# A new table of places, zero products and first-batch order for a two-layer transformer kernel, and GpSimd's clearing ahead of its first statistics

## The reference, cut to what matters

```python
h = _layernorm(x) * (1 + ca) + sa
x = x + ga * _L0_attn_ref(h, ...)      # scores masked to 0 above the diagonal; a score of 0 becomes NEG_FILL
h = _layernorm(x) * (1 + cb) + sb
x = x + gb * _L0_ffn_ref(h, ...)       # softmax gate, argmax, one of 8 experts, relu
h = _layernorm(x) * (1 + ca) + sa
x = x + ga * _L1_attn_ref(h, ...)      # 16 heads of 8: softmax(q k^T) v, then Wout
h = _layernorm(x) * (1 + cb) + sb
x = x + gb * _L1_ffn_ref(h, ...)       # W1, W2, no activation between
```

## Time and profile before

| | us |
|---|---|
| median of 3 runs | 1714.44 (1712.82 to 1715.45) |
| the profiled execution's own time | 1714.09 |
| its span, first to last instruction | 1712.8 |
| first row maximum (h = -32) | 129.74 |
| first exponential (h = 0) | 177.97 |

### The profile page before, as it was taken

The page is one execution under the profiler, slowest core; times in us unless marked ns, Lnnn a source line. Parts: engine busy times, 40 slices in busy tenths (PEclk is TensorE's granted clock), DMA queues, the critical chain, the costliest instruction groups (busy, mean ns, idle before and its releaser), DMA issues.

```text
span 1712.8 us, 56705 instructions
## 1 busy us (share of the span) xinstructions
PE 1621.6 (95%) x24168; PEld 707.5 (41%) x24168; DVE 1482.1 (87%) x2256; ACT 1368.1 (80%) x1934; POOL 667.8 (39%) x1085
## 2 busy tenths in 40 slices
PE   6998999999999999999999999999999999999998
PEld 3754443344434443334434443334434443323335
DVE  5649988999889998899889998899989998989963
ACT  4443778988899878988899878988899887777784
POOL 2321345445444355444554365344554362102010
PEclk9999999999999999999999999999999999999999
DMA  2111211112120311012110311112110221111101
GB/s 74 52 56 36 63 32 55 33 53 65 56 64 19 97 57 55 28 45 76 58 58 19 89 49 55 46 47 77 42 58 23 74 58 42 52 33 46 37 27 32
DMA packets 83288, 87.22 MB, mean 51 GB/s; under 512 B 9452, under 2 KB 67484, under 8 KB 83036
## 3 DMA queue, kind: packets, MB, share of 16 engines
q1 hardware_dynamic: 82492, 83.07, 16.4%
q10 hardware_dynamic: 544, 0.52, 0.1%
HBM read 61.02 MB, written 21.99 MB: 48 GB/s over the span
## 4 chain that ended last, share of the span: by engine, by line
PE 63%; ACT 16%; DVE 14%; issue 4%; POOL 2%; DMA 1%; SPq 0%; ACTq 0%; POOLq 0%; DVEq 0%
PE pv_psum L809 21%; PE side_psum L537 15%; PE buffer L794 11%; ACT p L1040 10%; DVE row_max L1364 8%; PE buffer L784 7%; PE side_psum L627 2%; PE buffer L537 2%; PE side_psum L594 1%; PE pv_psum L819 1%; ACT o_sb L1049 1%; DVE st_f L1103 1%; ACT p0T L967 1%; POOL sm_f L1394 1%; POOL xn_f L1400 1%
## 5 line engine op out<-in xcount | busy, mean ns | idle before, releaser
L1364 DVE TENSOR_REDUCE row_max<-buffer 128x2 f32<-128x1024 f32 x1024 | 1219.6, 1217 | 118.7 <-PE buffer L784 107.0
L1040 ACT ACTIVATE p<-buffer 128x1024 f32<-128x1024 f32 x1024 | 1043.6, 1026 | 184.2 <-PE buffer L794 171.5
L809 PE MATMUL pv_psum<-p,v 128*9 128x256 f32 x8192 | 575.7, 382 | 4.1 <-ACT o_sb L1049 2.2
L784 PE MATMUL buffer<-k_ops,q_ops 24*128 24x512 f16 x2048 | 397.6, 385 | 29.5 <-ACT p L1040 22.0
L794 PE MATMUL buffer<-q_ops,k_ops 26*128 26x512 f16 x2048 | 397.1, 385 | 4.4 <-DVE row_max L1364 3.1
L809 PEld LDWEIGHTS pv_psum<-p,v 128*9 128x9 f32 x8192 | 155.2, 89 | 234.9 <-issue 150.2
L794 PEld LDWEIGHTS buffer<-q_ops,k_ops 26*128 26x128 f16 x2048 | 96.0, 91 | 350.9 <-issue 244.4
L784 PEld LDWEIGHTS buffer<-k_ops,q_ops 24*128 24x128 f16 x2048 | 96.0, 91 | 147.7 <-ACT p L1040 112.3
L1510 POOL TENSOR_SCALAR nm_parts<-nm 128x16 f16<-128x16 f32 x64 | 17.0, 266 | 351.3 <-DVE nm L1287 351.3
L1495 POOL TENSOR_TENSOR hm<-masks,hT_f 128x1024 f32<-128x1024 bf16 x56 | 120.1, 2150 | 64.0 <-PE side_psum L537 50.8
L537 PE MATMUL side_psum<-we,hm 128*32 128x128 f32 x3648 | 121.0, 274 | 0.0
(11 more groups left out here) (310 smaller groups left out, 1674.5 us busy)
## 6 DMA issues: line engine op xcount, KB each, us to landing
masks<-masks_rows SPq DMA_DIRECT2D x16, 1024.0 KB, 5.7
q_ops<-products SPq DMA_DIRECT2D x256, 48.0 KB
k_ops<-products SPq DMA_DIRECT2D x256, 48.0 KB
attention<-o_sb SPq DMA_DIRECT2D x248, 18.0 KB
x<-in_L_attn_inputs SPq DMA_DIRECT2D x8, 512.0 KB, 4.3
products<-q_parts SPq DMA_DIRECT2D x16, 256.0 KB, 2.2
w_sb<-in_L_ffn_W SPq DMA_DIRECT2D x16, 256.0 KB, 3.2
out<-x SPq DMA_DIRECT2D x16, 256.0 KB, 2.8
```

The lines of the kernel that those rows point to most:

```text
L784: m = e.matmul(buffer[:, hh, :], q_ops[rows, slot, of, i * P:(i + 1) * P], k_ops[rows, slot, of, halves(half)[1]], start=True, stop=True)
L809: m = e.matmul(pv_psum[q:q + VW, half * QUARTER:(half + 1) * QUARTER], v1[b % 2][:, kb, 2 * hp + hh, :], p_sb[n % KEPT][:, hh, part * QUAR ...
L1040: e.activation(p_sb[n % KEPT][:, :, :], unit("exp", n)[0][:, :, :], ACT.Exp, scale=over_scale[n // (2 * PERIOD)]).then_inc(S["exp_done"], 1)
L1364: e.tensor_reduce(mx[pair % 2][:, :, i, half], unit("max", n)[0][:, :, :], axis=AX.X, op=ALU.max).then_inc(S["max_done"], 1)
```

## The change

Only tables change, and the place of four memsets. COUNTED has new values throughout (126 entries before, 122 now); of the other tables these lines show the pattern:

```diff
-SWITCH, LIGHT = 1.2, 6.6
+SWITCH, LIGHT = 0.6, 5.4
 PLACES = """
--15 maxima 0, -7 nm_split 0, -10 nm 0, 0 maxima 1, 1 nm_split 1, 4 nm 1, ...
+-14 maxima 0, -15 nm_split 0, -10 nm 0, 2 maxima 1, -3 nm_split 1, 6 nm 1, ...
...
 ALONE = """
-apply 0 0 1, channels 0 0 0, channels 0 0 1, g0 0 0, gates 0, g0 0 1, ...
+apply 0 0 1, channels 0 0 0, stats 0 0 1 0, channels 0 0 1, gates 0, g0 0 0, g0 0 1, ...
...
@@ gpsimd_program @@
+        for v in (be3[:, :], onehotT[:, :], b2_sb[:, :], gate_sb[:, :, :]):
+            e.memset(v, 0.0).then_inc(S["zero_rows"], 1)
+
         def norm_small(mv, sm, half, signal):
...
-        for v in (be3[:, :], onehotT[:, :], b2_sb[:, :], gate_sb[:, :, :]):
-            e.memset(v, 0.0).then_inc(S["zero_rows"], 1)
         pool.wait_ge(S["in_c"], 48)
```

More of the change, by code:

```diff
@@ L110 @@
 PLACES = """
[L111 to L114, removed]
@@ new lines @@
+3, -112 residual 0 0, -100 stats 0 2 0 0, -99 stats 0 2 0 1, -97 apply 0 2 0, -93 channels 0 2 0, -91 qk1 0 0 0, -64 parts 0 0 0, -85 qk1 0 1 0, -86
+parts 0 1 0, -88 v1 0 0, -133 stats 0 1 1 0, -132 stats 0 1 1 1, -132 apply 0 1 1, -127 channels 0 1 1, -126 wg 0 1, -125 top 0 1 0, -123 top 0 1 1,
+-124 index 0 1 0, -119 index 0 1 1, -118 gating 0 1 0, -119 onehot 0 1, -116 gating 0 1 1, -117 onehotT 0 1, -116 over_gating 0 1, -119 masks_out 0 1,
+-117 masks_load 0 1, -105 hm 0 4, -100 hm 0 5, -100 moe_a 0 4, -99 moe 0 4, -98 hm 0 6, -95 moe_a 0 5, -94 moe 0 5, -83 hm 0 7, -82 moe_a 0 6, -81 moe
@@ L177 @@
-1, index 0 0 0, squares 0, apply 1 0 0, index 0 0 1, times_v 0 7, onehot 0 0, up 0 1, stats 0 1 1 0, gating 0 0 1, stats 0 1 1 1, onehotT 0 0,
-channels 0 1 1, channels 1 0 0, apply 0 1 1, wg 0 1, hm 0 0, limits 0, top 0 1 0, apply 1 0 1, channels 1 0 1, moe_a 0 0, g0 1 0, masks_out 0 0,
-gating 0 1 0, inverse 0, g0 1 1, onehotT 0 1, gating 0 1 1, over_gating 0 0, index 0 1 0, moe 0 0, masks_load 0 0, top 0 1 1, hm 0 1, moe_a 0 1, index
-0 1 1, powers 0, later 1, onehot 0 1, moe 0 1, hm 0 2, hm 0 3, residual 0 0, masks_out 0 1, moe_a 0 2, moe 0 2, masks_load 0 1, moe_a 0 3, moe 0 3,
@@ new lines @@
+exp0 0 6, apply 0 1 0, masks_out 0 0, times_v 0 5, softmax 0 7, scores 0 7 1, transpose_p 0 6 0, channels 0 1 0, transpose_p 0 6 1, stats 1 0 0 0, wg
+0 0, top 0 0 0, stats 1 0 0 1, sums0 0 1, exp0 0 7, times_v 0 6, stats 1 0 1 0, transpose_p 0 7 0, top 0 0 1, index 0 0 0, squares 0, transpose_p 0 7
+1, times_v 0 7, gating 0 0 0, index 0 0 1, gating 0 0 1, onehot 0 0, stats 1 0 1 1, up 0 1, onehotT 0 0, apply 1 0 0, limits 0, channels 0 1 1, stats
+0 1 1 0, channels 1 0 0, channels 1 0 1, g0 1 0, stats 0 1 1 1, apply 0 1 1, apply 1 0 1, gating 0 1 0, inverse 0, hm 0 0, powers 0, wg 0 1, g0 1 1,
@@ new lines @@
+top 0 1 0, index 0 1 0, moe_a 0 0, onehotT 0 1, hm 0 1, top 0 1 1, over_gating 0 0, gating 0 1 1, moe 0 0, v0 1, moe_a 0 1, index 0 1 1, onehot 0 1,
+moe 0 1, hm 0 2, hm 0 3, hm 0 4, residual 0 0, later 1, gates 1, scores 1 0 0, moe_a 0 2, moe 0 2, moe_a 0 3, moe 0 3, stats 0 2 0 0, masks_load 0 0,
+stats 0 2 0 1, moe_a 0 4, hm 0 5, hm 0 6, over_gating 0 1, moe 0 4, softmax 1 0, exp0 1 0, moe_a 0 5, moe 0 5, apply 0 2 0, channels 0 2 0, qk1 0 0 0,
+hm 0 7, masks_out 0 1, moe_a 0 6, moe 0 6, scores 1 1 0, qk1 0 1 0, moe_a 0 7, masks_load 0 1, softmax 1 1, parts 0 0 0, parts 0 1 0, moe 0 7,
@@ L187, in make_plan @@
+transpose_p 1 0 0, scores 1 2 0, exp0 1 1, residual 0 1, v1 0 0, exp0 1 2, transpose_p 1 1 0, stats 0 2 1 0, softmax 1 2, times_v 1 0, channels 0 2 1,
+stats 0 2 1 1, qk1 0 0 1, v1 0 1, qk1 0 1 1, apply 0 2 1, scores 1 3 0, scores 1 4 0, exp0 1 3, parts 0 0 1, parts 0 1 1"""
 def make_plan():
```

50 lines of the change are left out of this document (22 added, 28 removed), and 37 rows, old and new, of tables (COUNTED, ZEROS_AHEAD, ZEROS_BESIDE).

## The result

The changed kernel takes 1720.74 us in the median of five runs (1718.19 to 1725.77), against 1714.44: 6.3 us more. The ratio on record is 1.0052, with a 95% interval of 1.0037 to 1.0067; that of the two medians, 1.0037, lies at its lower end. Either way the kernel is slower. A second measurement of it on another chip gave 1.0039 (1.0024 to 1.0054), median 1718.88. The forecast was 1713.4, no change. 1720.74 lies just above the stated range, which ended at 1720.5, and the second median lies inside it; what both rule out is the forecast of no change.

What follows compares the result with a forecast made beforehand. PE, busy 95% of the span, was taken as the bound, with DVE also full in part of each batch. Terms 0 + 0.6 + 0.3 - 3.4 + 1.0 + 0 + 0.5 = -1.0 gave 1713.1, as median 1713.4; range 1704.5 to 1720.5 us.

Steps and rivals of the forecast that it cites:

- The first batch's order: Head: experts gain, `residual 0 1` near 106.2, queries' store at 118.1; +0.6 us taken, bounds -2.0 to +3.0.
- its eight tiles at 1.8: First batch's second-half experts: eight tiles at 1.8 us plus new zero products, the last ending near 105.6.
- The clearing: Head: four memsets move to where POOL waited for batch 0's statistics; 0 taken, 1 us either side.
- Steps -32 to 0: Before the loop: 30 more zero products, 3.4 us on PE, mostly in its free time; +0.3 taken, -1.3 to +1.7.
- Step 42: Each batch: a `values` unit moved here covers PE's 0.49 us wait; seven batches, -3.4 us, bounds -3.4 and 0.
- `maxima 7`, `over_gating`: Each batch: both move into the stretch where DVE is full; 0.15 to 0.2 us a batch, +1.0 taken.
- rival (2): Step 100: eighth pair's split too late, up to 0.7 us a batch, 1719.0; 0.22 shared with strong (3), head's worse bound.
- The rule that the prediction cites: VectorE and GpSimd share a port pair; only VectorE operations in two-port mode or with two SBUF inputs hold it.
- Rival (3): Step 10: `ngmx` behind third `hm` on POOL delays ACT's exponentials, 0.5 us a batch, 1716.9; strong form shares 0.22.
- The last two batches: Late steps: eight more sets of zero products at 0.19 us, 1.5 if PE has no gap; +0.5 taken.
- The tail: End: six fewer zero products before the last transposes, which DVE releases; 0 taken.

Runs made afterwards that it cites:

- the old head: First batch's order and its zero products (but for batch 7) as before the change; put back in the changed kernel: ratio 1.0024 to the kernel before.
- places and steady values alone: Kernel before with only the changed places and the changed values spread up to step 831: ratio 1.0001.
- the mended new head: New first-batch order, keys' stores ahead of the scores, both `stats` together: on the kernel before 1.0018; on the changed kernel with old values and sets from 832, 1.0026.

## Why the prediction was wrong, step by step

- **The first batch's order: the step that failed.** Much of it was right. The 54 zero products ended 1.4 us behind DVE's norm (62.40 + 1.25 = 63.65; transposes at 65.03; forecast 0.5 to 1.7), `powers` was not last, the one-hot ended at 77.20 (forecast 78.0). DVE and PE of after:

```profile
62.40 1.25 DVE L1117 TENSOR_SCALAR xn_f<-x,sm_f 128x128 f32<-128x128 f32 x4 [1.67 <-POOL sm_f L1400]
...
68.70 0.17 DVE L1195 TENSOR_SCALAR qk_scale<-most 128x16 uint32<-128x16 uint32 x1 [1.66 <-POOL most L1584]
...
76.94 0.26 DVE L1249 TENSOR_TENSOR onehot<-consts,eidx_f 128x96 bf16<-128x96 f32 x1
```

```profile
59.04 6.16 PE L822 MATMUL pv_psum<-zero,ident_bf 128*128 128x256 bf16 x54
65.03 0.60 PE L597 MATMUL buffer<-consts,xn_f 128*128 128x128 f32 x4
...
71.30 1.08 PE L540 MATMUL side_psum<-wg,hT_f 128*32 128x128 f32 x32
```

  Two steps failed behind that. First, the experts did not gain. From the end of the one-hot to `residual 0 1` it took 30.1 us before and 30.6 after; the forecast, with its eight tiles at 1.8, needs 28.2. So `residual 0 1` started at 107.83, not 106.2, and with the softmax, which the forecast had, the queries' store was late by 2.0, not 0.6. The zero products among the tiles are not what is new: from `g0 1 1` to `moe 0 7` there were 56 before, and there are 67 now. Second, the working followed the queries' store alone, because that was last before. The keys' store on ACT's queue, which had been issued together with SP's part, had moved behind two copies of scores that wait for PE, and was 2.4 us more; the sum has no term for it. The last 1.1 us, from the keys' loads to the first row maximum, lie within what two kernels with the same head differ by (7.13 and 8.25). Together +5.5 at the first row maximum for the +0.6 taken, beyond even the bound of +3. (The profile of before was the earliest of the nine with the old head, 129.74 to 133.96; by the medians, 135.4 of three for 131.2 of nine, it is +4.2.)
- **The clearing: right**, 0 for 0 (0.9999). In the kernel with the clearing alone, SP's second group of loads went at 4.88 for 10.64, and the norm's four operations took 1.10 for 1.93, as forecast.
- **Steps -32 to 0: right in size** (48.48 for 48.23 to 48.37 with one dip in it, +0.2 for +0.3), which was in part luck: the products kept PE busy 2 us more, and a dip disappeared beside that, of which the sum knew nothing.
- **Step 42: wrong.** "Two steps earlier the unit covered nothing" failed. It covered 0.36 us there, and the way from one group of transposes to the next stayed 5.21 us: the gain was nothing that can be seen, not 3.4. The row at step 40 showed no idle time before, and I took that for a place without a wait, where it was a place with a covered wait. The 0.49 us also stood in six batches (1 to 6), not seven.
- **`maxima 7`, `over_gating` and rival (2): +1.0 taken, none seen.** Batches 2 to 5 were 0.98 shorter in all, and 0.8 in the kernel with places and steady values alone. The split met its step with time to spare. DVE, POOL and PE of after at steps 99 and 100, which answer to the earlier trace rows:

```profile
1112.59 0.17 DVE L1290 TENSOR_REDUCE nm<-row_max 128x16 f32<-128x32 f32 x1
```

```profile
1112.86 0.20 POOL L1516 TENSOR_SCALAR nm_parts<-nm 128x16 f16<-128x16 f32 x1 [6.58 <-DVE nm L1290]
...
1113.31 0.22 POOL L1518 TENSOR_TENSOR nm_parts<-nm_r,nm_parts 128x16 f16<-128x16 f32 x1
```

```profile
1114.60 0.23 PE L693 MATMUL side_psum<-ident_half,nm_parts 128*32 128x128 f16 x1 [0.15 <-DVE x L1222]
```

  The split was done at 1113.53, 1.07 us ahead of the transpose, for the 0.6 forecast. PE stood 0.15 us there, but for L1222, which empties the side bank. The first operation took 0.20, not 0.85; in before it took 0.84 to 0.85 in six batches, each time with the softmax operation L1210 already running, and in after never over 0.22 in all 64. The rule that the prediction cites from the Trainium skill, page SBUF — State Buffer, section "SBUF: two separate sides", is not tested by these rows: DVE was idle beside the first operation, and the third started 0.11 us ahead of L1222, which reads one tile from PSUM.
- **Rival (3): did not come.** `ngmx` ran at 976.64 right behind the third `hm` (974.52 + 2.14), and ACT's gating at 976.93 had no idle time before it; ACT came from exponentials that ended at 976.92.
- **The last two batches: wrong in size and reason.** +0.5 was taken for eight more sets at 0.19. The stretch grew by 1.7 us, and the ratio by 0.0021, by where values and sets stand; sets alone, put back, shortened nothing (250.05 for 249.34).
- **The tail: right**, 16.74 for 16.74.

So the direction was missed by the head (+5.5 for +0.6), the step-42 term (0 for -3.4) and the late steps (+1.7 for +0.5). What stays open: why the expert tiles came no closer together, and 3 to 4 us that the mended new head costs (1.0018 against 1, and 1.0026 against 1.0003), of which the first row maximum shows 0.8 to 1.4. In its profiles the loop loses another 0.2 to 0.8 us each near steps 784 and 832, and 0.4 near 152 in two of three pairs, at instructions that are the same; why was not settled.

## What to carry to other kernels

When an order moves stages, list for the transfer that ends a chain every queue that issues a part of it, and what stands ahead of it on each; the part that was last before is not the part that is last after. A unit of work that is taken from a step without idle time has to be asked what it was covering there. Filler that keeps the clock up costs its time on the path and gives some of it back as clock: compare stretches only at equal numbers of dips, and read a ratio beside the mean clock of its runs.

## What the runs showed of the hardware

- A dip of the granted clock to 0.5 (1.2 of 2.4 GHz) mostly lasts 3.4 us, some last 6.8 and one of these profiles has one of 23.9. One of 3.4 us costs about 1.2 us of this kernel, by a line through the runs; that goes with most of the scatter between the runs of one kernel (1708.78 at a mean clock of 0.998, 1717.11 at 0.993).
- Dips come back at the same places in different profiles of kernels that agree there: near 20, 96 and 161 in the kernels with the old head and old zero products. In one pair of profiles, 30 zero products fewer in the steps under 0 went with a new dip at 162.
- The same loads landed very differently: from the start of the keys' loads to the first row maximum it took 6.1 to 8.8 us in eighteen profiles, 7.13 and 8.25 in two kernels with the same head. The same store of queries took 2.1 us in seventeen profiles and 4.2 in one, and ACT's store of keys 2.5 us when it was issued together with SP's part (3.5 in one profile), and 3.8 to 4.8 when it was issued 2.1 us later.
- A DMA that ACT issues stands in ACT's own queue: with two copies ahead of it that waited for PE it went 2.1 us behind the part that SP issued (123.28 and 121.18), without them at the same time (122.84).
- A GpSimd operation that takes 0.20 us took 0.84 to 0.85 in six of 64 places, each time with a VectorE softmax operation on two SBUF tiles already running.
